# Attention block of a recurrent layer: the first group's k and q rows loaded inside the projection, and VectorE's small sums with one operand in PSUM

## What is computed

```python
xn = layernorm(x)
q = rope((xn @ wq.T))   # 32 heads of 32
k = rope((xn @ wk.T))   # 8 heads of 32, each used by 4 query heads
v = (xn @ wv.T)
y = softmax(q k^T / sqrt(32) + causal mask) v     # 4 batches
s = y @ wo.T
thought = layer_norm(xn, in_g, in_b)[:, -1, :] @ agg_w + agg_b     # (4, 1024)
for _ in range(4):
    t = layer_norm(thought, pn_g, pn_b)
    t = gelu(t @ d1_w + d1_b)                     # (4, 4096)
    thought = thought + (t @ d2_w + d2_b)
gate = sigmoid(xn @ gate_w + gate_b)
f = layer_norm(xn + gate * (thought @ bc_w + bc_b)[:, None, :], out_g, out_b)
out = x + s * silu(f)
```

## Time and profile before

| | |
|---|---|
| median of three runs | 2590.91 us (2590.49 to 2593.19) |
| the profiled execution's own time | 2590.74 us |
| its span in the profile | 2589.1 us |
| TensorE matmul, busy | 2493.8 us, 96% |
| VectorE busy | 1730.7 us, 67% |
| ScalarE busy | 980.8 us, 38% |
| GpSimd busy | 1368.0 us, 53% |
| mean granted TensorE clock | 0.985 |

### The profile page before, as it was taken

How to read it: one execution, slowest core, us unless ns; L and a number is a source line. 1 busy time by engine, 2 the same in 40 slices (tenths; PEclk the granted TensorE clock), 3 DMA queues, 4 the chain that set the end, 5 groups by cost and what they waited for, 6 DMA issues and landing times. The chain is left out here.

```text
span 2589.1 us, 43561 instructions
## 1 busy us (share of the span) xinstructions
PE 2493.8 (96%) x14180; PEld 1684.1 (65%) x14180; DVE 1730.7 (67%) x3500; ACT 980.8 (38%) x1645; POOL 1368.0 (53%) x637
## 2 busy tenths in 40 slices
PE   5999999996999999999999999999899999999998
PEld 4888888884555545554455545555378888888886
DVE  6444555444777777777777787777477777777777
ACT  2111111110666655666566656666431111111111
POOL 1122221122999989999899989999711111111111
PEclk9999999997999999999999999999999999999999
DMA  6544444537665665566466556555475666666666
GB/s 243 187 164 151 158 162 176 187 139 240 200 189 164 190 189 166 181 192 206 130 196 194 164 172 199 167 181 183 169 195 108 129 119 120 117 118 119 121 121 122
DMA packets 228017, 428.90 MB, mean 166 GB/s; under 512 B 16836, under 2 KB 99780, under 8 KB 227928
## 3 DMA queue, kind: packets, MB, share of 16 engines
q1 hardware_dynamic: 154536, 375.85, 43.7%
q0 software_dynamic: 73392, 51.91, 13.4%
HBM read 313.67 MB, written 113.51 MB: 165 GB/s over the span
## 5 line engine op out<-in xcount | busy, mean ns | idle before, releaser
L934 DVE CUSTOM_DVE_ANT_0 bcast<-mxp,mask_q 128x128 f32<-128x128 f32 (+7 forms) x1024 | 726.2, 753 | 307.1 <-PE mxp L1041 172.8
L855 ACT ACTIVATE pr<-stp 128x512 f32<-128x512 f32 x1152 | 649.5, 595 | 492.8 <-PE stp L1050 367.7
L1050 PE MATMUL stp<-qs,ks 97*128 97x512 f32 x1152 | 479.0, 454 | 3.5 <-ACT pr L855 2.7
L466 PE MATMUL eo<-xt,w 128*128 128x512 f32 x1920 | 448.8, 393 | 3.6 <-DVE xt L383 3.6
L804 POOL TENSOR_TENSOR acc<-acc,pr 128x2048 f32<-128x2048 f32 x96 | 440.8, 4592 | 4.4 <-POOL acc L804 3.8
L466 PEld LDWEIGHTS eo<-xt,w 128*128 128x128 f32 x1920 | 358.5, 189 | 77.2 <-issue 4.0
L1050 PEld LDWEIGHTS stp<-qs,ks 97*128 97x128 f32 x1152 | 209.4, 189 | 247.1 <-ACT pr L855 116.0
L1419 PE MATMUL gp<-g,xa 128*128 128x512 f32 x1536 | 357.1, 392 | 11.6 <-DVE g L1357 8.2
L1419 PE MATMUL op<-o,ya 128*128 128x512 f32 x1536 | 353.6, 390 | 0.8 <-DVE ya L1407 0.8
L1419 PEld LDWEIGHTS gp<-g,xa 128*128 128x128 f32 x1536 | 290.8, 189 | 72.8 <-DVE g L1357 8.5
L1419 PEld LDWEIGHTS op<-o,ya 128*128 128x128 f32 x1536 | 288.3, 188 | 61.3 <-DVE ya L1407 1.7
(11 more groups left out here) (148 smaller groups left out, 3057.3 us busy)
## 6 DMA issues: line engine op xcount, KB each, us to landing
wch<-in_d_w SPq DMA_DIRECT2D x132, 1024.0 KB, 9.4
qs<-q_scratch SPq DMA_DIRECT2D x192, 256.0 KB, 7.9
xa<-xt_scratch POOLq DMA_DIRECT2D x66, 512.0 KB, 6.1
xt_scratch<-xt SPq DMA_DIRECT2D x16, 2048.0 KB, 14.1
q_scratch<-r SPq DMA_DIRECT2D x64, 512.0 KB, 3.6
yr<-y_scratch POOLq DMA_DIRECT2D x33, 512.0 KB, 5.8
xs<-in_x SPq DMA_DIRECT2D x33, 512.0 KB, 5.5
y_scratch<-ys SPq DMA_DIRECT2D x65, 256.0 KB, 2.1
```

Of the source, the lines that this page charges most:

```text
L466: last = nc.tensor.matmul(out, lhs[a](k), rhs[c](k), start=(k == 0 and (a, c) == (0, 0)), stop=(k == KT - 1 and (a, c) == (1, 0)))
L855: nc.scalar.activation(pr[half][:, :, at:at + P], stp[u % 2][:].rearrange("p (h t) -> p h t", h=REP), ACT.Exp, scale=SCALE).then_inc(act_d ...
L934: last = nc.vector.tensor_tensor_reduce(out=bcast[:, k % 2, hh * step:hh * step + w], in0=mxp[k % 2][:, hh * step + c0:hh * step + c0 + w] ...
L1050: last = nc.tensor.matmul(bank, ks[par][:, j * P:(j + 1) * P], qs[par][:, i // 4, :, (i % 4) * P:(i % 4 + 1) * P], start=True, stop=i != j)
```

## The change

The first group's rows. A new tensor `shared`, 128 x 2 x 8 x 512, is allocated outside the three parts. In the projection its halves are `xt[0][0]` and `xt[1][0]`, the buffers of the even halves. In the attention part it holds q of even groups (`qs0`), both k buffers and `xa`; in the output part `ya`, `xa` and four of the eight blocks of `o2`. During the projection's last half (n = 7, whose x lies in the other buffers) SyncE's queue loads group 0's k and q with eight transfers behind the three small rows and ahead of the half's stores, after waits for the stores of half 6 and for its v products. The prologue doesn't load them any more, and VectorE raises the semaphores in their place.

The small sums. `chunk_out` is two additions, each with one operand in PSUM and one in SBUF, in place of two reductions and an addition of two SBUF operands. The addition of d2_b to `th` moves from VectorE (L1013) to GpSimd's `ln_pool`. The squares move from VectorE (L908) to ScalarE, in the slot behind `lc`; VectorE's sum of the squares gets an entry of its own, `lq`, behind `mx 10` in slot 22, and waits there for ScalarE.

The rest of the diff hands the slices of `shared` to the output part in place of tensors of its own. The core of the diff:

```diff
-22: rc 0, mx 10
+22: rc 0, mx 10, lq
...
         xlt = osb("xlt", [P, KT, B], F32)
+        shared = osb("shared", [P, 2, KT, HALF], F32R)
+        front, rest = (shared[:, i].rearrange("p k t -> p (k t)") for i in range(2))
+        qs0 = front[0:3 * HD + 1, :].rearrange("p (a h t) -> p a h t", a=2, h=REP)
+        ks = [rest[0:3 * HD + 1, i * T:(i + 1) * T] for i in range(2)]
+        xa = [rest[:, (2 + i) * T:(3 + i) * T].rearrange("p (k t) -> p k t", k=KT) for i in range(2)]
+        ya = [front[:, i * T:(i + 1) * T].rearrange("p (k t) -> p k t", k=KT) for i in range(2)]
+        o2_last = [front[:, 2 * T:3 * T], front[:, 3 * T:4 * T], rest[:, 0:T], rest[:, T:2 * T]]
...
-        xt = [[sb(f"xt{p}{i}", [P, KT, HALF], F32R) for i in range(2)] for p in range(2)]
+        xt = [[shared[:, p], sb(f"xt{p}1", [P, KT, HALF], F32R)[:]] for p in range(2)]
...
+            def first_group():
+                for p0, np_, part in ((0, 2 * HD, slice(0, 2)), (2 * HD, HD, slice(0, 1))):
+                    sp.dma_start(f32(ks0[p0:p0 + np_]), k_d[0, part].rearrange("r e (f g) t -> (r e f) g t", g=KV)
+                                 [:, 0, :]).then_inc(first_in, 16)
+                for h in range(2):
+                    for p0, part in ((0, 0), (HD, 0), (2 * HD, 1)):
+                        sp.dma_start(f32(qs0[p0:p0 + HD, h]), q_d[0, part].rearrange("e (f g) t -> (e f) g t", g=2 * REP)
+                                     [:, 0:REP, h * HALF:(h + 1) * HALF]).then_inc(first_in, 16)
...
                         for dst, v in ((gl, in_g), (bl, in_b)):
                             sp.dma_start(dst, v.partition_broadcast(B)).then_inc(gb_in, 16)
+                        sp.wait_ge(xt_out[0], 32 * B + 1)
+                        sp.wait_ge(v_done, 4 * (NB - 1))
+                        sp.wait_ge(r_out, 32 * NP * (NB - 1) + 1)
+                        first_group()
...
+            sp.wait_ge(first_in, 16 * 8)
...
-            load_k(0, 0)
-            load_q(0, 0, 0)
-            load_q(1, 0, 0)
             load_w(0, whole(agg_w))
...
                 nc.gpsimd.tensor_tensor(rs[:], ve[:], mhalf[:], ALU.pow).then_inc(ln_rs, 1)
+                nc.gpsimd.tensor_tensor(th, th, fvec[:, 3, :].unsqueeze(2).to_broadcast([P, KT, B]), ALU.add)
...
+            def squares(tu):
+                act.wait_ge(tr_free, tu + 2)
+                nc.scalar.activation(sq[:], cen[:], ACT.Square).then_inc(sq_done, 1)
...
+                        elif e[0] == "lc" and "l0" in use:
+                            squares(tb + use["l0"])
...
-            def layernorm_centre(tu, base):
+            def layernorm_centre(tu):
                 dve.wait_ge(tr_full, tu + 1)
                 nc.vector.tensor_tensor(cen[:], th, rows(trp[:, 0:B]), ALU.subtract).then_inc(tr_free, 1)
-                dve.wait_ge(tr_free, tu + 2)
-                link(nc.vector.tensor_tensor(sq[:], cen[:], cen[:], ALU.mult), base)
+
+            def layernorm_squares(k):
+                dve.wait_ge(sq_done, k + 1)
                 nc.vector.tensor_reduce(s2[:], sq[:].rearrange("p k r -> p r k"), AX.X, ALU.add).then_inc(ln_sum, 1)
...
-            def chunk_out(tu, base):
-
+            def chunk_out(tu, into, base, addend):
                 dve.wait_ge(tr_full, tu + 1)
                 v = trp[:].rearrange("p (c n k r) -> p n c r k", c=4, n=2, k=2)
-                for nb in range(2):
-                    last = nc.vector.tensor_reduce(fr[:, 4 * nb:4 * nb + 4, :], v[:, nb, :, 0:B, :], AX.X, ALU.add)
-                last.then_inc(tr_free, 1)
-                dve.wait_ge(tr_free, tu + 2)
+                link(nc.vector.tensor_tensor(four(fr[:]), v[:, :, :, 0:B, 0], four(addend), ALU.add), base)
+                return nc.vector.tensor_tensor(four(into), v[:, :, :, 0:B, 1], four(fr[:]), ALU.add)
...
-                                nc.vector.tensor_tensor(hpre[:], fr[:], bc(b1c[:], B), ALU.add).then_inc(hp_done, 1)
+                                chunk_out(tu, hpre[:], base, bc(b1c[:], B)).then_inc(tr_free, 1)
+                                dve.wait_ge(tr_free, tu + 2)
+                                dve.sem_inc(hp_done, 1)
                             else:
-                                link(nc.vector.tensor_tensor(th, th, fr[:], ALU.add), base)
+                                chunk_out(tu, th, base, th).then_inc(tr_free, 1)
+                                dve.wait_ge(tr_free, tu + 2)
...
                         elif e[0] == "ls" and "l0" in use:
-                            link(nc.vector.tensor_tensor(th, th, bc(fvec[:, 3, :], B), ALU.add), base)
                             layernorm_sum()
...
+                        elif e[0] == "lq" and "l1" in use:
+                            layernorm_squares(s + 1)
```

More of the change, by code:

```diff
@@ L242, in turn @@
                         sp.dma_start(xt_d[bass.ds(b, 1), p, :, :, half * HALF:(half + 1) * HALF]
-                                     .rearrange("a p k t -> (a p) k t"), f32(xt[p][half][:])).then_inc(xt_out[half], 16)
+                                     .rearrange("a p k t -> (a p) k t"), f32(xt[p][half])).then_inc(xt_out[half], 16)
                     if final and half:
@@ L536, in sem @@
             return ctx.enter_context(nc.semaphore(name))
-        qs = [sb(f"qs{i}", [QR + 1, 2, REP, HALF], F32R) for i in range(2)]
-        ks = [sb(f"ks{i}", [QR + 1, T], F32R) for i in range(2)]
+        qs = [qs0, sb("qs1", [QR + 1, 2, REP, HALF], F32R)]
         vs = [sb(f"vs{i}", [P, NT, HD], F32) for i in range(2)]
@@ L814, in _ @@
             for part in range(2):
-                nc.gpsimd.dma_start(xa[part][:], xt_d[0, part, :, :, 0:P]).then_inc(x0_in, 16)
+                nc.gpsimd.dma_start(xa[part], xt_d[0, part, :, :, 0:P]).then_inc(x0_in, 16)
             turns(pool, turn)
@@ L836, in copy_y @@
                 nc.scalar.activation(ys[half][:], yp[:], ACT.Copy).then_inc(ys_done, 1)
+            def squares(tu):
+                act.wait_ge(tr_free, tu + 2)
+                nc.scalar.activation(sq[:], cen[:], ACT.Square).then_inc(sq_done, 1)
             max_rows(0, 1)
             copy_burst(2)
+            squares(5)
             def turn(s, c, par, use, left=3):
@@ L1249, in output_phase @@
         g1, g2 = (sb(f"g{i}", [P, KT, D], F32R) for i in (1, 2))
-        o1, o2 = (sb(f"o{i}", [P, KT, D], F32R) for i in (1, 2))
-        ya = [sb(f"ya{i}", [P, KT, P], F32R) for i in range(2)]
-        yr = sb("yr", [P, KT, P], F32)
-        xs = [sb(f"xs{i}", [P, D], F32) for i in range(2)]
+        o1 = sb("o1", [P, KT, D], F32R)
+        o2 = sb("o2", [P, KT // 2, D], F32R)
+        blocks = lambda w: [w[:, k, :] for k in range(KT)]
+        g1, g2, o1 = blocks(g1), blocks(g2), blocks(o1)
+        o2 = [o2[:, k, :] for k in range(KT // 2)] + o2_last
+        yr = sb("yr", [P, KT, P], F32)[:]
+        xs = [sb(f"xs{i}", [P, D], F32)[:] for i in range(2)]
         wst = [wch[k // 2 % 2][:, 2 * (k // 4) + k % 2, :] for k in range(KT)]
@@ L1306, in load_xa @@
                 for part in range(2):
-                    nc.gpsimd.dma_start(xa[part][:], xt_d[bass.ds(nn // NT, 1), part, :, :, bass.ds((nn % NT) * P, P)]
+                    nc.gpsimd.dma_start(xa[part], xt_d[bass.ds(nn // NT, 1), part, :, :, bass.ds((nn % NT) * P, P)]
                                         .rearrange("a p k t -> (a p) k t")).then_inc(xa_in, 16)
@@ L1334, in _ @@
                     act.wait_ge(w_in[k], 16)
-                nc.scalar.activation(w1[:, k, :], wst[k], ACT.Copy).then_inc(w1_done, 1)
+                nc.scalar.activation(w1[k], wst[k], ACT.Copy).then_inc(w1_done, 1)
                 if n == YA_AT:
                     act.wait_ge(ya_in, 16)
-                    nc.scalar.activation(ya[0][:], yr[:], ACT.Copy).then_inc(y1_done, 1)
+                    nc.scalar.activation(ya[0], yr, ACT.Copy).then_inc(y1_done, 1)
             with act.Fori(0, TILES // 2) as m:
@@ L1418, in product @@
                             cols = slice(half * HALF, (half + 1) * HALF)
-                            last = nc.tensor.matmul(bank[:, cols], lhs[pa][:, k, :], ws[pw][:, k, cols],
+                            last = nc.tensor.matmul(bank[:, cols], lhs[pa][:, k, :], ws[pw][k][:, cols],
                                                     start=(k == 0 and (pa, pw) == (0, 0)),
```

52 lines of the change are left out of this document (28 added, 24 removed).

## The result

The changed kernel takes **2550.73 us** (median of 4 runs, 2549.78 to 2551.92), and the kernel before takes 2591.91 in the same comparison (2590.49 to 2593.19): a ratio of 0.984, 95% interval 0.982 to 0.986.

What follows compares the result with a forecast made beforehand. TensorE was busy for 96% of the span, so time could be won only where it idled or ran at its lower clock. Gains of 8.7 + 21.8 + 0.4 = 30.9 us from 2590.74 gave 2560 us, range 2552 to 2570.

Steps and rivals of the forecast that it cites:

- Part A: Boundary and prologue: early rows bring the first maximum forward and remove a later transfer wait; 7.5 + 1.5 - 0.3 = 8.7 us gained.
- The wait for agg_w: Prologue: TensorE's 1.80 us wait for this 4 MB load goes, since its transfers are issued earlier; 1.5 us gained.
- The squares' round trip: First layer norm in the prologue: VectorE waits for ScalarE's squares; 0.3 us lost, between 0 and 1.28.
- Part B: Three step ends (turns 7, 15, 23): their 25.0 us excess goes except 3 x 1.05; 21.8 us gained.
- residual: Each step end: two means on TensorE, 0.35 each, and a new wait before ss 0; 1.05 us, between 0 and 4.
- Part C: Other turns: the addition to th shortens in 13 odd turns; 0.4 us gained, between 0 and 2.0.
- (1): Step ends: a new wait, with TensorE's clock falling, keeps half of the 25 us; 2570 us, chance 0.08.
- (2): Prologue: held by agg_w or the small vectors behind it; gain 4.1 instead of 9.0, 2565 us, chance 0.08.
- (3): Prologue and step ends: squares need another table set, two loads of 1.28 us per call; 2562 us, chance 0.05.
- (4): All 32 turns: sums with a PSUM operand wait for GpSimd too; 208 us slower, about 2790, chance 0.02.
- (5): Block opening and sums: something else delays the block equally and the sums still stall; 2590 us, chance 0.01.

Runs made afterwards that it cites:

- experiment 6: The changed kernel with two extra reductions on VectorE, results unused, behind the sum of each odd turn; 2560.73 us.
- experiment 10: The kernel before with only the new form of the chunk sum, bias and squares staying on VectorE, rows loaded in the prologue; 2557.80 us.
- experiment 1: The changed kernel with all small sums, bias addition and squares as before, so only the early rows remain; 2581.78 us.
- experiment 3: The changed kernel with the first group's rows loaded in the prologue again, plus three increments of an unused semaphore on VectorE; 2558.46 us.
- Experiment 12: The changed kernel with centring ahead of the tenth maximum, t_in copied later in the prologue, and TensorE's awaited increments first on VectorE; 2547.32 us.
- Experiment 8: The changed kernel with the step ends' bias addition (d2_b to th) on VectorE again, from two SBUF operands; 2551.47 us.
- Experiment 9: The changed kernel with the squares on VectorE again, directly behind the centring; 2550.38 us.
- Experiment 4: The changed kernel with the old sum in odd turns only: two reductions and an addition of two SBUF operands; 2562.52 us.
- experiment 5: The changed kernel with the old form of the sum in the even turns only; 2555.45 us.
- experiment 2: The changed kernel with the first group's rows loaded in the prologue again, so only the sums remain; 2573.12 us.

## Why the prediction was right and wrong

**Part A held at the boundary, and the match of the sum, 8.6 against 8.7, is partly luck.** From the end of the v product to the first maximum the time fell from 14.26 to 6.32 us, by 7.9 where 7.5 was said, and TensorE waited for VectorE's increments as said. All nine kernels with the early rows are at 5.7 to 6.3 us there, the five without them at 14.3 to 15.1.

The prologue from there to turn 0 went from 41.19 to 39.25, by 1.9, where 1.5 - 0.3 was said, and this is not shown to be the change's doing. The four other kernels that load the rows as before take 37.4 to 39.0, and those with early rows 37.0 to 39.4; experiment 6, whose code ahead of turn 0 is that of the changed kernel, takes 37.06. The length goes with the clock: it stood at 0.50 for 28.5 us of this stretch in the kernel before, for 27.0 in the changed one and for 20.8 in experiment 6. The wait for agg_w fell away, but it is absent in experiment 10 as well, which loads the rows as before. The squares' round trip cost 0.05 us instead of 0.3: TensorE waits 0.95 us for the sum behind them, where it waited 0.90 before. Against all this stands 1.2 us by which the projection ended later in this execution; that too is no effect that can be told, for in the five kernels without early rows it ends between 595.8 and 597.2, and in the nine with them between 596.0 and 597.1. Measured by kernels that differ in little else, the early rows are worth 10 us beside the old sums (experiment 1) and 7.7 beside the new ones (experiment 3 against the changed kernel; 8.6 if each is taken against its own runs of the kernel before).

**Part B held in size, 19.6 against 21.8, and failed in two of its three reasons.** The size was the excess of the earlier trace rows less a residual. The residual came out at 1.6 to 1.7 us for each step end where 1.05 was taken (and 0.5 once, in turn 9): ss 0 waits 1.06 us for the centring, not 0.3. VectorE was as early as the working had it: the centring ends 16.2 us after the turn's first maximum, where 16.4 was said. TensorE was earlier. In turn 5 before, ss 0 starts 851.78 - 836.05 = 15.73 us after the first maximum, in the changed kernel's turn 5 at 840.76 - 825.79 = 14.97: the 0.76 us are the two short waits of part C, which lie ahead of it and which the working had left in. Experiment 12 shows that the wait for the centring was worth 0.75 a step end. The reasons given were that L1013 and L908 leave VectorE, and in third place that the state is added with a PSUM operand; only the third was needed. Experiments 8 and 9 put each of them back, and the time did not move; experiment 10 left both there and still had the step ends at 38.5, 0.2 above the changed kernel's. L1013 was slow only because the slow chunk sum ahead of it delayed it to 0.24 us behind the start of GpSimd's addition. The three edits were costed as one sum and one price, which hid that one was enough.

**Part C is the step that failed: 12.0 against 0.4** (and, as just shown, it made part B's residual too small as well). Two things in it were wrong. The first is the view. The prediction took TensorE's waits that can be put down to the addition as 16.1 - 14.1 = 2.0 us, from the matmuls' waits of the earlier trace rows; the weight loads on the same line waited for 9.9 us beyond the step ends. A weight load that comes late makes its matmul late, but the matmul's own row then shows no wait for VectorE. The second is the argument that pairs with a short addition were as long as the others. It rested on turn 9, which has the addition of 0.46 us but is long for another reason: none of the weight loads of L1037 waits for VectorE in it, but TensorE waits 0.64 us for a small transfer, and in the changed kernel, where all additions are short, it does so again for 0.51 us and the turn is at 37.19. The row of each, before and after:

```profile
995.58 0.50 PE L1050 MATMUL stp<-qs,ks 97*128 97x512 f32 x1 [0.64 <-DMA qs<-mt]
```

```profile
978.77 0.49 PE L1082 MATMUL stp<-qs,shared 97*128 97x512 f32 x1 [0.51 <-DMA qs<-mt]
```

The other short one, 0.82 us in turn 11, has an even turn beside it that is 0.37 us longer, with its own addition at 1.03 us. Experiments 4, 10 and 6 show the cause of the other odd turns' length. Undoing the odd turns' sum gives back 11.8 us, the new form alone shortens the odd turns fully, and a dose of other work lengthens them by what exceeds a margin of 0.3 us. The addition of 1.19 us with the two reductions before it makes the next maximum 1.08 us late, 0.77 past that margin. With 12.0 in place of 0.4 the sum of the prediction is 8.7 + 21.8 + 12.0 = 42.5, 3 over the profile's 39.5, and those 3 are the residual (2.2) and the end of the kernel (0.8).

**The rivals.** (1), a new wait at the step ends, was there in kind and cost 2.2 us more than the forecast's residual, not 12.5. (2) did not come: TensorE waits for no transfer in the prologue. (3) did not come: the square took 0.23 us between exponentials with no table load. (4) and (5) did not come. The PSUM form never waited: 0.18 to 0.19 us under a running addition of 4.56. On this the Trainium skill (Perfetto Trace Analysis, Optimizing Scalar/DVE Operations) had some 65 ns more for a PSUM operand; the trace has 0.19 us with a PSUM operand and 0.19 with two of SBUF, so the measurement decides against it for this size. The Trainium skill (SBUF — State Buffer, SBUF: two separate sides) has VectorE and GpSimd lock a shared pair of ports for a whole instruction, and a VectorE instruction with two SBUF inputs among those that take it when GpSimd's reads SBUF; the trace agrees, with 4.32 us for the addition that starts 0.24 us behind GpSimd's, and 0.19 to 0.22 for the same one 0.92 us ahead of it.

**The range** was built from the bounds of the terms, and the bound of part C, 2.0 us, was itself read from the wrong rows, so that no reaching to it could have held the result.

## What to carry to other kernels

Price a late engine from the weight loads' waits as well as the matmuls', and take the bound of a term from the length of the turns (odd 37.4 against even 36.65 stood in the trace before) rather than from a list of waits. Where one engine's instruction can hold up another's, as here, an instruction's duration is a property of its start time: look for the first late instruction of the chain, since the slow one behind it may be cured by curing the first. Before several cures are credited with a sum, put each back by itself.

## What the runs showed of the hardware beyond that

- The same VectorE addition of 128x32, two SBUF operands, took 4.31 to 4.34 us or 0.19 to 0.22, by a shift of some 1.2 us against GpSimd. With the odd turns cured, the even turns' addition, where it was kept, was dearer (1154 ns in the median instead of 316, experiment 5).
- VectorE can stand still for 7.5 us with no semaphore to wait for, twice in one execution (14.3 us of the time), and three more instructions at the head of its program remove it (experiments 2 and 3); the cause stays open. A kernel that only loses a few instructions can be slowed by this, and a comparison with it credits the wrong part.
- A pause of TensorE of 4.93 us at the boundary still left its clock at 0.50 until 616.8 and for 13.6 us after 623.6, while from 637.2 to 1828.5, where its longest wait is 1.2 us, it stayed at 1.00. In the kernel before, each of the three waits of 4.7 us had 6.8 us at 0.50 with it, which began during the wait, and turn 15 another 3.4 us.
